# Row maxima of an attention kernel: split into two 16-bit parts before the turn instead of after it, and two casts one slot later

## The reference

```python
def attn(x):                                   # x is layer-normed
    q, k, v = proj(Wq, bq), proj(Wk, bk), proj(Wv, bv)          # (B, H, S, 16)
    s = einsum('bhqd,bhkd->bhqk', q, k) / sqrt(16)
    decay = sum_n softmax(mix)[h, n] * clip(dp, .01, .9999)[h, n] ** abs(tq - tk)   # n = 0, 1
    p = softmax(s * decay, axis=-1)
    return einsum('bhqk,bhkd->bhqd', p, v) @ Wo.T + bo
x = x + attn(layernorm(x))
x = x + ffn(layernorm(x))    # two matmuls with ternary weights, ReLU between them
```

## Time and profile before

| what | before |
|---|---|
| median of 3 runs | 1883.89 us |
| the profiled execution, its own time | 1886.52 us |
| its span (first to last instruction) | 1884.7 us |
| PE busy | 1772.6 us, 94% |
| DVE busy | 1584.5 us, 84% |
| ACT busy | 1327.7 us, 70% |
| POOL busy | 781.1 us, 41% |
| first and last turn L1084 | 177.6 and 1663.7 us, 64 of them |

### The profile page before, as it was taken

One profiled execution on the slowest core, in us unless ns is written; L12 is line 12 of the kernel. 1 busy time (PEld: TensorE's weight loads), 2 busy tenths in 40 slices (PEclk: granted clock), 3 DMA queues, 4 the chain that ended last, 5 costly groups with the idle time before them and its releaser, 6 DMA issues. The chain is left out here.

```text
span 1884.7 us, 32075 instructions
## 1 busy us (share of the span) xinstructions
PE 1772.6 (94%) x11794; PEld 787.5 (42%) x11794; DVE 1584.5 (84%) x3768; ACT 1327.7 (70%) x1518; POOL 781.1 (41%) x403
## 2 busy tenths in 40 slices
PE   6747999999999999999999999999999999985998
PEld 4422444444444444444444444444444444423666
DVE  5667898989898989898989898989898989955785
ACT  2343868686868686868686868686868686672555
POOL 3040909090909090909090909090909090011010
PEclk9875999999999999999999999999999999997999
DMA  6988263636364636363636363636363734307531
GB/s 125 281 266 195 68 157 94 157 93 157 94 157 95 157 95 156 94 157 94 157 93 157 94 156 95 157 95 157 94 157 93 158 93 112 108 21 192 143 93 34
DMA packets 132441, 242.61 MB, mean 129 GB/s; under 512 B 27696, under 2 KB 62896, under 8 KB 122032
## 3 DMA queue, kind: packets, MB, share of 16 engines
q1 hardware_dynamic: 129376, 237.84, 51.7%
q0 software_dynamic: 560, 2.36, 1.3%
q10 hardware_dynamic: 2352, 0.40, 0.1%
HBM read 69.08 MB, written 44.56 MB: 60 GB/s over the span
## 5 line engine op out<-in xcount | busy, mean ns | idle before, releaser
L933 ACT ACTIVATE probs<-tile 128x1024 f32<-128x1024 f32 x1024 | 1000.3, 1023 | 309.5 <-PE tile L1098 164.4
L960 DVE TENSOR_REDUCE part_max<-ring 128x1 f32<-128x512 f32 x1536 | 964.1, 682 | 131.1 <-PE ring L1070 131.1
L1070 PE MATMUL ring<-k_stack,q_stack 96*128 96x512 f16 (+2 forms) x3072 | 715.1, 314 | 25.7 <-DMA q_stack<-lo 16.5
L1101 PE MATMUL tile<-q_stack,k_stack 98*128 98x512 f16 (+2 forms) x2560 | 585.3, 326 | 0.5 <-ACT probs L933 0.2
L1117 PE MATMUL acc<-probs,v_ones 128*32 128x512 f32 x4096 | 546.1, 605 | 0.0
L1070 PEld LDWEIGHTS ring<-k_stack,q_stack 96*128 96x128 f16 x3072 | 265.9, 99 | 531.7 <-DVE part_max L960 386.2
L870 POOL TENSOR_TENSOR diag<-diag,row_max 128x1024 f32<-128x1024 f32 x64 | 121.5, 1899 | 615.9 <-DVE row_max L973 615.9
L1101 PEld LDWEIGHTS tile<-q_stack,k_stack 98*128 98x128 f16 x2560 | 249.5, 98 | 277.4 <-ACT probs L933 8.1
L176 POOL TENSOR_TENSOR decayed<-qk,table_in 128x1024 f32<-128x1024 f32 x128 | 305.5, 2394 | 91.0 <-DMA table_in<-table_scratch 77.5
L962 DVE TENSOR_REDUCE part_max<-ring 128x1 f32<-128x384 f32 x512 | 279.1, 545 | 8.5 <-PE ring L1070 8.5
L190 POOL TENSOR_TENSOR lo<-decayed,hi 128x1024 f16<-128x1024 f32 x120 | 255.5, 2134 | 0.0
(11 more groups left out here) (142 smaller groups left out, 974.4 us busy)
## 6 DMA issues: line engine op xcount, KB each, us to landing
q_stack<-hi SPq DMA_DIRECT2D x320, 128.0 KB, 3.8
k_stack<-hi SPq DMA_DIRECT2D x128, 256.0 KB, 4.3
q_stack<-lo SPq DMA_DIRECT2D x160, 128.0 KB, 3.0
table_in<-table_scratch SPq DMA_DIRECT2D x64, 256.0 KB, 8.4
k_stack<-lo SPq DMA_DIRECT2D x64, 256.0 KB, 3.8
out_scratch<-heads_out SPq DMA_DIRECT2D x64, 256.0 KB, 2.9
v_scratch<-v_out SPq DMA_DIRECT2D x8, 1024.0 KB, 6.8
q_scratch<-q_out SPq DMA_DIRECT2D x32, 256.0 KB, 4.0
```

What stands on the lines that cost most here:

```text
L933: nc.scalar.activation(probs[:, t % 4], tile[t % 2][:].rearrange("p a b -> p (a b)"), ACT.Exp, scale=1.0 / (SCALE * SCALE * HEAD_DIM ** 0. ...
L960: nc.vector.tensor_reduce(out[:, k:k + 1], ring_bank(n), AX.X, ALU.max).then_inc(ring_free, 1)
L1070: last = nc.tensor.matmul(ring[:, n % RING, col:col + width], q_stack[h][0:STACK, q // UNIT_SLOTS, level, q0:q0 + P], k_stack[h][0:STACK, ...
L1101: last = nc.tensor.matmul(out, k_stack[h][:, level, kb * P:(kb + 1) * P], q_stack[h][:, half, level, col:col + width], start=bank not in s ...
```

## The change

Two edits.

1. The split is done before the turn. After L973 DVE does two small operations on 128 x 8 in SBUF: `tensor_scalar` writes the 16-bit part into `max_parts[:, 0]`, and after a semaphore `scalar_tensor_tensor` reads `row_max` and that part and writes the rest into `max_parts[:, 1]`. ACT repeats `max_parts` instead of `row_max`, into a 16-bit `max_repeated`. The turn becomes a 16-bit matmul with the 16-bit identity. Behind it DVE takes the turned rows with one copy, which also frees the bank (`take_max`); SP waits for that copy by `ring_free`. POOL's subtraction still waits for L973 alone.
2. `hi_slot`: the casts of chunks 8 and 9 stand in slots 13 and 15 instead of 12 and 14.

```diff
-        max_repeated = sb("max_repeated", [P, MAXROWS * RAW, UNIT_SLOTS])
+        max_parts = sb("max_parts", [P, MAXROWS, UNIT_SLOTS], F16)
+        max_repeated = sb("max_repeated", [P, MAXROWS, RAW, UNIT_SLOTS], F16)
...
-        hi_slot = (0, 1, 3, 4, 6, 8, 9, 11, 12, 14)
+        hi_slot = (0, 1, 3, 4, 6, 8, 9, 11, 13, 15)
...
-            def store_max_rows(h, half, count):
-
-                sp.wait_ge(rows_ready, count)
+            def store_max_rows(h, half, taken):
+
+                sp.wait_ge(ring_free, taken)
...
-            def repeat_max(par, count):
-
-                act.wait_ge(max_ready, count)
-                nc.scalar.copy(max_repeated[:], row_max[:, par].unsqueeze(1).broadcast_to([P, MAXROWS * RAW, UNIT_SLOTS])
+            def repeat_max(count):
+
+                act.wait_ge(parts_ready, count)
+                nc.scalar.copy(max_repeated[:], max_parts[:].unsqueeze(2).broadcast_to([P, MAXROWS, RAW, UNIT_SLOTS])
                                ).then_inc(repeated_ready, 1)
...
-            def split_max(slot, unit_count, more=True, o=0):
+            def split_max(par, unit):
+                dve.wait_ge(max_ready, unit + 1)
+                if unit >= 1:
+                    dve.wait_ge(repeated_ready, unit)
+                nc.vector.tensor_scalar(max_parts[:, 0], row_max[:, par], -1.0 / MAXUNIT, None, ALU.mult
+                                        ).then_inc(high_ready, 1)
+                dve.wait_ge(high_ready, unit + 1)
+                nc.vector.scalar_tensor_tensor(out=max_parts[:, 1], in0=row_max[:, par], scalar=-1.0 / MAXUNIT,
+                                               in1=max_parts[:, 0], op0=ALU.mult,
+                                               op1=ALU.subtract).then_inc(parts_ready, 1)
+
+            def take_max(slot, unit_count, more=True, o=0):
...
-                src = ring_bank(n)[0:MAXROWS * LO_ROWS, 0:P]
-                nc.vector.tensor_scalar(max_rows[:], src, -1.0 / MAXUNIT, None, ALU.mult).then_inc(max_seen, 1)
-                dve.wait_ge(max_seen, (unit_count if unit_count is not None else 0) + 1)
-                nc.vector.scalar_tensor_tensor(out=max_rows[LO_ROWS:], in0=src[LO_ROWS:], scalar=-1.0 / MAXUNIT,
-                                               in1=max_rows[LO_ROWS:], op0=ALU.mult,
-                                               op1=ALU.subtract).then_inc(rows_ready, 1)
-                nc.vector.tensor_copy(scrap[:], src[0:UNIT_SLOTS, 0:1]).then_inc(ring_free, 1)
+                nc.vector.tensor_copy(max_rows[:], ring_bank(n)[0:MAXROWS * LO_ROWS, 0:P]).then_inc(ring_free, 1)
...
                         finish_max(u % 2, seen, UNITS * i + u)
+                        split_max(u % 2, UNITS * i + u)
                     if s % UNIT_SLOTS == TURN_SLOT:
-                        split_max(s, UNITS * i + u, more, o)
+                        take_max(s, UNITS * i + u, more, o)
...
-                nc.tensor.transpose(ring[0:MAXROWS * LO_ROWS, n % RING, 0:P],
-                                    max_repeated[:].rearrange("p r b -> p (r b)"), ident[:]).then_inc(ring_full, 1)
+                nc.tensor.matmul(ring[0:MAXROWS * LO_ROWS, n % RING, 0:P], max_repeated[:].rearrange("p m r b -> p (m r b)"),
+                                 keep["ident16"][:], start=True, stop=True, skip_group_check=True).then_inc(ring_full, 1)
```

More of the change, by code:

```diff
@@ L630, in turn_item, with turn_taken @@
     return ring_item(slot, ITEMS) if more or slot < SLOTS - LEAD else ring_item(SLOTS - LEAD, 0)
+def turn_taken(slot, more, o):
+    return RING_STEP * o + turn_item(slot, more) + AHEAD_ITEMS + 1
 def score_parts(block, side):
@@ L666, in attention_block @@
         row_max = sb("row_max", [P, 2, UNIT_SLOTS])
-        max_repeated = sb("max_repeated", [P, MAXROWS * RAW, UNIT_SLOTS])
+        max_parts = sb("max_parts", [P, MAXROWS, UNIT_SLOTS], F16)
+        max_repeated = sb("max_repeated", [P, MAXROWS, RAW, UNIT_SLOTS], F16)
         max_rows = sb("max_rows", [MAXROWS * RAW * UNIT_SLOTS, P], F16)
-        scrap = sb("scrap", [UNIT_SLOTS, 1])
         unit = sb("unit", [P, 1])
@@ L690, in attention_block @@
         blocks_seen = sem("blocks_seen")
-        max_ready, max_seen = sem("max_ready"), sem("max_seen")
+        max_ready, high_ready, parts_ready = sem("max_ready"), sem("high_ready"), sem("parts_ready")
         repeated_ready = sem("repeated_ready")
-        rows_ready, rows_in = sem("rows_ready"), sem("rows_in")
+        rows_in = sem("rows_in")
         diag_ready = sem("diag_ready")
@@ L792, in _ @@
             builder.load(sp, 1)
-            store_max_rows(0, 0, 1)
+            store_max_rows(0, 0, turn_taken(TURN_SLOT - UNIT_SLOTS, True, 0))
             def step(i, o, more):
@@ L804, in step @@
                     store_out(i - 1, UNITS - 1)
-                store_max_rows(0, 1, UNITS * i + 2)
+                store_max_rows(0, 1, turn_taken(TURN_SLOT, more, o))
                 if o == STEPS - 1:
@@ L819, in step @@
                     load_q(0, 0, 0)
-                store_max_rows(1, 0, UNITS * i + 3)
+                store_max_rows(1, 0, turn_taken(UNIT_SLOTS + TURN_SLOT, more, o))
                 if more:
@@ L832, in step @@
                     load_v(0, i + 1)
-                store_max_rows(1, 1, UNITS * i + 4)
+                store_max_rows(1, 1, turn_taken(2 * UNIT_SLOTS + TURN_SLOT, more, o))
                 if i + 2 < STEPS:
@@ L843, in step @@
                         load_q(1, 0, x)
-                    store_max_rows(0, 0, UNITS * i + 5)
+                    store_max_rows(0, 0, turn_taken(3 * UNIT_SLOTS + TURN_SLOT, more, o))
                 if o == STEPS - 1:
@@ L908, in _ @@
                                ).then_inc(const_ready, 1)
-            def repeat_max(par, count):
-                act.wait_ge(max_ready, count)
-                nc.scalar.copy(max_repeated[:], row_max[:, par].unsqueeze(1).broadcast_to([P, MAXROWS * RAW, UNIT_SLOTS])
+            def repeat_max(count):
+                act.wait_ge(parts_ready, count)
+                nc.scalar.copy(max_repeated[:], max_parts[:].unsqueeze(2).broadcast_to([P, MAXROWS, RAW, UNIT_SLOTS])
                                ).then_inc(repeated_ready, 1)
             nc.scalar.activation(warm[:], ident[:, 0:1], ACT.Exp)
-            repeat_max(0, 1)
+            repeat_max(1)
             act.sem_inc(exp_done, 2)
@@ L930, in step @@
                         if s % UNIT_SLOTS == TURN_SLOT and t % 2 and (more or u < UNITS):
-                            repeat_max(u % 2, UNITS * i + u + 1)
+                            repeat_max(UNITS * i + u + 1)
                         act.wait_ge(tile_full, EXPS * o + t + 1)
@@ L1020, in _ @@
                     finish_max(0, s + LEAD + 1, None)
+                    split_max(0, 0)
                 if s % UNIT_SLOTS == TURN_SLOT and s + LEAD >= UNIT_SLOTS:
-                    split_max(s, None)
+                    take_max(s, None)
             def step(i, o, more):
```

## The result

| what | before | after |
|---|---|---|
| median | 1884.29 us | 2017.03 us |
| ratio of the times | | 1.0701, 95% interval 1.0686 to 1.0716 |
| the profiled execution, its own time and span | 1886.52, 1884.7 | 2018.46, 2016.2 |
| PE busy | 1772.6 (94%) | 1814.5 (90%) |
| DVE busy | 1584.5 (84%) | 1697.0 (84%) |

The time came 132.7 us over before; 108.8 were forecast (1992), and 2017 lies in the range, near its upper end. One execution of the changed kernel's six (9718.55 us) and one of e2's five (5716.07 us, the profiled one) were in a slow state whose cause is not known: the ratios leave them out (the other five of the changed kernel have a median of 2016.45), and e2 has no trace to compare with the others.

The account below looks back on a forecast made before the run. PE was taken as the bound, DVE close behind. The four handovers add 6.95 us a step, times 15 = 104.3, plus 2.9 in the last step and 1.6 ahead of the first: 108.8 over 1883.9, forecast 1992, range 1955 to 2022.

Parts of the forecast that it names:

- The block of the two instructions: Behind L973, both stand for POOL: scalar_tensor_tensor about 1.8 us at every handover, tensor_scalar about 1.6 in slot 5.
- rival 2: At every handover the second new instruction slips in ahead of POOL's subtraction; 1892 us, chance 0.08.
- Handover C: Slot 21: one block makes the first reduction 1.86 us late; net +1.53 a step.
- B and D: Handovers of slots 13 and 29: one block each, costing 1.58 us against 0.50 and 0.24 before.
- The turn's 0.06: At each handover, the 16-bit turn's 128 columns were taken to cost 0.06 us.
- B's single block: Slot 13: POOL is done with chunk 8's product and idle by 0.8 us, so one block; +1.08 a step.
- The last step and the prologue: Last step +2.9 us, without POOL builder work; the handover ahead of the first step +1.6 us.
- Handover A: Slot 5: POOL's remainder, then its subtraction, block the two instructions; first reduction 3.33 us late, +3.00 a step.
- rival 4: A second block in slot 13, +24 us, 2017; or PE's clock falls because of the gaps; chance 0.07.
- Rival 1: No block at any handover, since neither instruction takes what POOL needs; 14 to 16 us gained, 1869, chance 0.06.
- Rival 3: Only the instruction with two SBUF inputs is blocked, the 16-bit tensor_scalar is not; +81 us, 1965, chance 0.09.
- The moved casts: Slot 13: the late copy behind slot 12's cast goes, 0.26 us; moving chunk 9's cast lets nothing wait.

Follow-up runs that it names:

- e2: The changed kernel with the casts of chunks 8 and 9 back in slots 12 and 14; 2015.60 us, ratio 1.0695 to the kernel before.
- e3: The changed kernel, but POOL's subtraction waits for both parts instead of row_max; 1895.25 us, ratio 1.0057 to the kernel before.
- e6: The changed kernel with the scalar_tensor_tensor replaced by a one-input reduction of the identity's columns; 1895.48 us, ratio 1.0055 to the kernel before.
- e7: The changed kernel with the tensor_scalar replaced by a one-input reduction, the second instruction keeping the whole maximum in 16 bits; 1958.47 us, ratio 1.0390.
- e4: The changed kernel with POOL's remainder of chunk 2 moved behind the subtraction at slot 5's handover; 1965.93 us, ratio 1.0429 to the kernel before.
- e9: The changed kernel with POOL's subtraction waiting for both parts, and POOL's work and the casts reordered; 1876.01 us, ratio 0.9952 to the kernel before.
- e11: e9 with the 16-bit turn's weights widened from 64 to 128 columns, the new ones zero; 1870.35 us, ratio 0.9924 to the kernel before.
- e1: The kernel before with only the casts of chunks 8 and 9 moved to slots 13 and 15; 1881.04 us, ratio 0.9982.
- e10: e9 with the turn in 32 bits again; 1872.44 us, ratio 0.9934 to the kernel before.

## Why the prediction was right, and where not, step by step

**The block of the two instructions**: right. Forecast 0.16 and about 1.8 at C, 1.6 and 1.8 at A; measured 0.17 and 1.76, 1.58 and 1.81. e3 takes the block away with one wait and gets 122 us back, and e6 and e7 show that each instruction waits by itself. Whether POOL's L875 keeps its place between the two was rival 2's point of decision; it came in between in all 64 handovers. The section "Who interferes with whom" of the Trainium skill's page "SBUF — State Buffer" states such a block for both forms: for `tensor_scalar` in a two-port mode, and for a VectorE instruction with two SBUF inputs while GpSimd reads SBUF. The runs agree: for the second 1758 ns beside POOL and 168 without, for the first 1.58 us and 172 ns. One reading in the prediction was too wide: not all reductions of the kernel before read the ring. L973 has its input and its output in SBUF, runs wholly inside an instruction of POOL in 30 handovers (860.51 in the earlier trace rows, L190 from 860.16 in the earlier trace rows) and takes 0.19 all the same; e6's reduction does too.

**Handover C**: forecast 1.84, measured 1.71. The first reduction starts at 977.78, 0.08 before the instruction ahead of it ends, where I had put 0.03 behind it, so 0.11 of the 0.13 is there. The same 0.12 to 0.13 is in B and D (1.58 forecast, 1.46 measured) and in A. Together -0.50 a step, -7.5. Three signs were off with it: PE waits 1.21 at item 3 of C and 0.95 at B and D, where I had about 1.5, and the item behind the turn starts 0.18 after it and not within 0.1. The turn's 0.06 was too small a term, but in the changed kernel it costs little: item 1 behind the turn waits for DVE in any case.

**B's single block**: right. POOL was idle 0.82 us there, 0.8 were forecast, and e4 shows the edge of it: there POOL's product of chunk 8 ends 0.18 behind L978, and B costs 1.51 instead of 1.46.

**The last step and the prologue**: 2.9 and 1.6 forecast; in the traces the last step is 2.7 longer and the first products start 1.8 later. The second says little, since their start varies by over 3 us from kernel to kernel.

**Handover A is the step that failed.** Forecast 3.31, measured 4.62 in the median step. Without the clock C's 1.71 and the 1.47 more of lateness make 3.18, and the half clock adds 1.44. The sum had no term for the clock. I had named a fall of it in rival 4, without a price, and argued it away by the busy share over a whole step, nine tenths. That average hid what mattered: the clock falls at the end of one gap of 2.69 us, and it does not at gaps of 1.21 (e4, and C of the changed kernel). In 10 of the 15 full steps the trace has the half clock for 3.4 us at A; in four it has it for 6.8, and A and the slots behind it cost 1.6 more. In the first it has it for 10.2, at a price of 4.5, but there the gap itself is 0.65 shorter. The clock: 10 x 1.44 + 4 x 3.04 + 4.5 = 31.1 us. Less the 7.5 from above and the 0.65 of the first step that is 22.9, and in the traces the 15 steps are 127.2 us longer, 22.9 over the forecast 104.3. The two medians differ by 1 us more than the two profiled executions.

**Rival 1 (no block, 1869)** did not come, and without the block the change as written would not reach its number either. Its gain was counted with a turn of 0.06, which the change does not have: with its narrow 16-bit turn e9 gets 1876, with the wide one e11 gets 1870. **Rival 4** has the measured number, 2017, by luck: that was its price for a second block at B, which did not come; its other half, the clock, did. The range reached to 2022 on account of that second block, so that it took in the clock's 31 us is luck too. **Rival 3 (only two inputs block, 1965)**: e7 is near its number but by another mechanism; the `tensor_scalar` with 16-bit output is blocked as well.

**The moved casts**: right that B's 0.26 goes (e1: 0.27) and that no keys come late.

## What to carry to other kernels

Before an instruction is moved from PSUM operands to SBUF operands, look what GpSimd runs at that moment: on 8 columns the move cost ten times the instruction (1.76 us against 0.17), nearly all of it the wait for GpSimd's instruction to end. If it must be there, order GpSimd behind it with a semaphore. When stalls are added up on TensorE, ask for the longest single gap, and price the clock behind it, not the mean busy share. And do not count on a smaller element type to make a small matmul cheaper: here the 16-bit turn took 0.17 where the 32-bit one took 0.14. Measure from start to start.

## What I had not expected of the hardware

A 16-bit turn with 64 columns of weights holds the next item up for 0.17 us, a 32-bit one with the same 64 columns for 0.14, and a 16-bit one with 128 columns for 0.07. At D in e9's trace the next weight load (PEld) starts 0.17 behind the start of the narrow 16-bit turn; in the kernel before it starts with the turn, and in e10 and e11 too, within 0.02. First e9, then before:

```profile
928.54 0.11 PEld L1082 LDWEIGHTS ring<-k_stack,q_stack 96*128 96x128 f16 x2
```

```profile
933.89 0.23 PEld L1070 LDWEIGHTS ring<-k_stack,q_stack 96*128 96x128 f16 x2
```

e11 against e9 shows that for the 16-bit turn the width of the weights decides this (the rows that it writes go from 64 to 128 with it); e10 shows that width alone does not, since 64 columns in 32 bits have it not. Why is open.

The clock is the second thing: it was down at the end of each of 14 gaps of 2.7 us and one of 2.0, for 3.4 to 10.2 us, and never at the gaps of 1.2 and less. Between 1.2 and 2.0 there was none, and why the shortest of the 15 had the longest stretch at the lower level is open.
